# The query bias of a linear attention: from two products per batch on TensorE to operands of the ScalarE and VectorE maps

## What is computed

```python
q = _heads(hidden_states @ q_w.T + q_b, b, s)
k = _heads(hidden_states @ k_w.T + k_b, b, s)
v = _heads(hidden_states @ v_w.T + v_b, b, s)
qp = jax.nn.elu(q) + 1.0
kp = jax.nn.elu(k) + 1.0
kv = jnp.einsum('bhsd,bhse->bhde', kp, v)
z = jnp.einsum('bhsd,bhd->bhs', qp, kp.sum(axis=2))[..., None]
attn = jnp.einsum('bhsd,bhde->bhse', qp, kv) / (z + EPS)
out = attn.transpose(0, 2, 1, 3).reshape(b, s, HID)
return out @ o_w.T + o_b
```

## Time and profile before

| what | us |
|---|---|
| median of 3 runs | 138.21 |
| lowest, highest | 137.30, 138.31 |
| the profiled execution's own time | 135.21 |
| its span | 133.4 |
| TensorE busy in the span | 125.2 |
| VectorE, ScalarE, GpSimd busy | 80.9, 75.8, 71.0 |

### The profile page before, as it was taken

The page is one execution under the profiler, slowest core; times in us unless marked ns, Lnnn a source line. Parts: engine busy times, 40 slices in busy tenths (PEclk is TensorE's granted clock), DMA queues, the critical chain, the costliest instruction groups (busy, mean ns, idle before and its releaser), DMA issues.

```text
span 133.4 us, 2624 instructions
## 1 busy us (share of the span) xinstructions
PE 125.2 (94%) x975; PEld 116.9 (88%) x975; DVE 80.9 (61%) x205; ACT 75.8 (57%) x162; POOL 71.0 (53%) x90
## 2 busy tenths in 40 slices
PE   6989797999899999999999999999999999999980
PEld 2249696999899999889999989999989999999980
DVE  0269985789986895857786696564635413324122
ACT  4168579595676589568543982654397530355300
POOL 3015999959999998855270352650226440144600
PEclk9999999999999999999999999999999999999999
DMA  3899976000000000000000200000200000200002
GB/s 69 231 387 374 396 244 227 5 0 2 2 5 0 0 2 5 0 0 0 5 0 0 79 0 5 2 0 0 82 1 0 2 0 5 79 0 0 5 0 79
DMA packets 4721, 7.64 MB, mean 57 GB/s; under 512 B 608, under 2 KB 2592, under 8 KB 4580
## 3 DMA queue, kind: packets, MB, share of 16 engines
q1 hardware_dynamic: 4478, 7.37, 16.1%
q10 hardware_dynamic: 230, 0.11, 0.5%
HBM read 6.42 MB, written 1.05 MB: 56 GB/s over the span
## 4 chain that ended last, share of the span: by engine, by line
PE 76%; DVE 6%; DMA 4%; SPq 3%; POOL 3%; ACT 2%; issue 2%; POOLq 0%; DVEq 0%
PE bank L1123 35%; PE bank L1136 17%; PE bank L1001 5%; PE bank L1087 4%; DMA at<-in_mask_key 4%; PE bank L1025 3%; PE bank L1109 3%; PE bank L1049 2%; PE bank L1059 2%; PE bank L1095 1%; PE bank L1069 1%; ACT mbias L396 1%; POOL at L280 1%; PE bank L992 1%; DVE st L647 1%
## 5 line engine op out<-in xcount | busy, mean ns | idle before, releaser
L1123 PE MATMUL bank<-xh_home,wug 128*128 128x256 f32 x384 | 49.5, 285 | 0.0
L1123 PEld LDWEIGHTS bank<-xh_home,wug 128*128 128x128 f32 x384 | 47.2, 190 | 0.5 <-issue 0.4
L311 POOL TENSOR_TENSOR hs<-front,hs 128x256 fp32r<-128x256 f32 x32 | 24.1, 761 | 32.6 <-ACT hs L530 32.6
L521 ACT ACTIVATE front<-bank,vecs 128x256 f32<-128x256 f32 x32 | 15.0, 473 | 18.6 <-PE bank L1123 18.5
L822 DVE SCALAR_TENSOR_TENSOR front<-bank,sc_up,front 128x256 f32<-128x256 f32 x32 | 15.2, 480 | 16.1 <-ACT front L521 16.1
L1136 PE MATMUL bank<-wdh,hs 128*128 128x256 f32 x192 | 23.8, 283 | 0.0
L1136 PEld LDWEIGHTS bank<-wdh,hs 128*128 128x128 f32 x192 | 23.4, 191 | 0.1
L530 ACT CAST hs<-front 128x256 fp32r<-128x256 f32 x32 | 12.8, 400 | 5.5 <-DVE front L822 5.4
L1025 PE MATMUL bank<-wqkv,xT 128*128 128x256 f32 x96 | 14.2, 289 | 0.0
L1025 PEld LDWEIGHTS bank<-wqkv,xT 128*128 128x128 f32 x96 | 12.3, 189 | 0.6 <-DVE xT L689 0.4
L647 DVE BATCH_NORM_STATS2 st<-x_res 128x6 f32<-128x256 f32 x24 | 9.1, 416 | 5.2 <-DMA x_res<-in_x 5.0
(11 more groups left out here) (105 smaller groups left out, 194.9 us busy)
## 6 DMA issues: line engine op xcount, KB each, us to landing
wd_a<-in_w_d SPq DMA_DIRECT2D x1, 1024.0 KB, 8.6
front<-in_w_ug SPq DMA_DIRECT2D x2, 512.0 KB, 9.8
back<-in_w_ug SPq DMA_DIRECT2D x2, 512.0 KB, 5.3
out<-x_res SPq DMA_DIRECT2D x8, 128.0 KB, 1.9
wd_b<-in_w_qkv SPq DMA_DIRECT2D x3, 256.0 KB, 5.6
x_res<-in_x SPq DMA_DIRECT2D x1, 512.0 KB, 6.8
back<-in_ctx_t SPq DMA_DIRECT2D x1, 260.0 KB
x_res<-in_x SPq DMA_DIRECT2D x2, 128.0 KB, 3.3
```

Source lines behind the costliest of these rows:

```text
L311: g.tensor_tensor(hs[:, 1, n % JB, :], sg[:, n % RING, :], hs[:, 0, n % JB, :].bitcast(F32), ALU.subtract)\
L521: a.activation(sg[:, n % RING, :], B("GU", n)[:, 0:SEQ], ACT.Silu, scale=vecs[:, V_WSUG + JB + j:V_WSUG + JB + j + 1]).then_inc(s["sg"], 1)
L1123: ins = mm(dst[:, n * SEQ:(n + 1) * SEQ], wug[:, wa, k, at_col + j * P:at_col + (j + 1) * P], xh[b][:, xb, k, :], start=(i == 0), stop=(i ...
```

## The change

The seventh product for each block of queries goes, and with it the query half of the bias rows and their split. The query bias arrives as two more columns of the tile `vecs`, and `vector_sums` on VectorE (which takes the place of `scale_up`, at an earlier point) makes two tiles of 128 x 2 from it, -q_b and q_b + 1. ScalarE now makes three instructions of `exp_q` instead of one: for each block m a Relu of -q - q_b from the bank into `eq`, then, after a wait for both, the exponential of the negated `eq` in place. This is exp(min(q + q_b, 0)). VectorE makes two instructions of `elu_q` instead of one: for each block m the maximum of `eq` and bank + (q_b + 1).

```diff
-V_SUG, V_SUD, V_WSUG, V_COLS = 0, 2, 10, 26
-
-K_COLS, Q_COLS = slice(0, HID), slice(HID, 2 * HID)
+V_SUG, V_SUD, V_WSUG, V_QB, V_COLS = 0, 2, 10, 26, 28
...
+        qb_minus = sb("qb_minus", [P, FB])
+        qb_plus = sb("qb_plus", [P, FB])
         rows = sb("rows", [P, 3, HID])
-        bias_r = sb("bias_r", [BIAS_ROWS, 2 * HID], F32R)
-        ones = sb("ones", [BIAS_ROWS, HID], F32R)
+        bias_r = sb("bias_r", [BIAS_ROWS, HID], F32R)
+        ones = sb("ones", [BIAS_ROWS, P], F32R)
...
-                a.activation(eq[:, :], B("Q", b)[:, :], ACT.Exp, bias=neg1[:, :]).then_inc(s["eq"], 1)
+                    act.wait_ge(s["q_bias"], 1)
+                for m in range(FB):
+                    cols = slice(m * SEQ, (m + 1) * SEQ)
+                    a.activation(eq[:, cols], B("Q", b)[:, cols], ACT.Relu, bias=qb_minus[:, m:m + 1], scale=-1.0).then_inc(s["q_neg"], 1)
+                act.wait_ge(s["q_neg"], FB * b + FB)
+                a.activation(eq[:, :], eq[:, :], ACT.Exp, scale=-1.0).then_inc(s["eq"], 1)
...
-            bias_hi(K_COLS)
+            bias_hi()
...
-            bias_hi(Q_COLS)
...
-                v.scalar_tensor_tensor(qT[:, b % 2, :, :], eq[:, :].rearrange("p (m s) -> p m s", m=FB), 1.0,
-                                       B("Q", b)[:, :].rearrange("p (m s) -> p m s", m=FB),
-                                       ALU.min, ALU.max).then_inc(read_of("Q", b), 1)
+                if b == 0:
+                    dve.wait_ge(s["q_bias"], 2)
+                for m in range(FB):
+                    cols = slice(m * SEQ, (m + 1) * SEQ)
+                    ins = v.scalar_tensor_tensor(qT[:, b % 2, m, :], B("Q", b)[:, cols], qb_plus[:, m:m + 1], eq[:, cols], ALU.add, ALU.max)
+                ins.then_inc(read_of("Q", b), 1)
...
-            def scale_up():
+            def vector_sums():
                 dve.wait_ge(ld["vec"], 16)
+                q_bias = vecs[:, V_QB:V_QB + FB]
+                v.tensor_scalar(qb_minus[:, :], q_bias, -1.0, None, ALU.mult).then_inc(s["q_bias"], 1)
+                v.tensor_scalar(qb_plus[:, :], q_bias, 1.0, None, ALU.add).then_inc(s["q_bias"], 1)
                 v.tensor_tensor(sc_up[:, :], vecs[:, V_WSUG:V_WSUG + JB], vecs[:, V_SUD:V_SUD + JB], ALU.mult).then_inc(s["sc_up"], 1)
...
-            bias_lo(0, K_COLS)
+            bias_lo()
             u_lo(0)
             xT_lo(0)
             w_lo(1)
             w_lo(2)
-            bias_lo(1, Q_COLS)
             ln_stats(1, 1)
+            vector_sums()
             elu_k(0)
             v_add(0)
             u_lo(1)
             ln_stats(1, 2)
-            scale_up()
             elu_q(0)
             xT_lo(1)
...
                 if b == 0:
                     pe.wait_ge(s["w_lo"], 3)
-                    pe.wait_ge(s["bias"], 2)
...
                     for n, (k, wa, xb) in enumerate(PASSES):
-                        mm(into, wqkv[:, wa, 2, k, m * P:(m + 1) * P], xT[:, b % 2, xb, k, :], start=(n == 0), stop=False)
-                    ins = mm(into, bias_r[:, HID + m * P:HID + (m + 1) * P], ones[:, :], start=False, stop=True)
+                        ins = mm(into, wqkv[:, wa, 2, k, m * P:(m + 1) * P], xT[:, b % 2, xb, k, :], start=(n == 0),
+                                 stop=(n == len(PASSES) - 1))
...
-        "bias": np.stack([b_kq, b_kq, np.ones(2 * HID, np.float32)]),
+        "bias": np.stack([b_k, b_k, np.ones(HID, np.float32)]),
...
-        "vec": np.concatenate([columns(a[n]) for n in ("L0_ffn_SU_ug", "L0_ffn_SU_dp", "L0_ffn_Wscale_ug")], 1),
+        "vec": np.concatenate([columns(a[n]) for n in ("L0_ffn_SU_ug", "L0_ffn_SU_dp", "L0_ffn_Wscale_ug", "L0_attn_q_b")], 1),
```

More of the change, by code:

```diff
@@ L178, in decoder_kernel @@
         qkv_raw = wd_b[:, 0:FB * 3, :].rearrange("p (c f) o -> p c f o", c=3)
-        bias_raw = kvs[0:BIAS_ROWS, :, :].rearrange("p b e -> p (b e)")[:, 0:2 * HID]
+        bias_raw = kvs[0:BIAS_ROWS, :, :].rearrange("p b e -> p (b e)")[:, 0:HID]
         bytes_of = at[:, :, :, :].rearrange("p two i d -> p (two i d)").bitcast(U8)
@@ L210, in decoder_kernel @@
                  "ug_hi ug_lo fly pre_hi pre_lo wd_hi "
-                 "xT_hi ek eq z_eps z_inv at_hi "
+                 "xT_hi ek q_neg eq q_bias z_eps z_inv at_hi "
                  "sx logit prob rsum x2 y "
@@ L379, in bias_rows @@
             def bias_rows():
-                a.mul(ones[:, :], neg1[0:BIAS_ROWS, :].to_broadcast([BIAS_ROWS, HID]), -1.0).then_inc(s["ones"], 1)
+                a.mul(ones[:, :], neg1[0:BIAS_ROWS, :].to_broadcast([BIAS_ROWS, P]), -1.0).then_inc(s["ones"], 1)
                 act.wait_ge(s["bias_zero"], 1)
@@ L418, in w_hi, with bias_hi @@
                 a.copy(wqkv[:, 0, c], qkv_raw[:, c]).then_inc(s["w_hi"], 1)
-            def bias_hi(cols):
+            def bias_hi():
                 act.wait_ge(ld["bias"], 16)
-                a.copy(bias_r[:, cols], bias_raw[:, cols]).then_inc(s["bias_hi"], 1)
+                a.copy(bias_r[:, :], bias_raw).then_inc(s["bias_hi"], 1)
             def normalise(n, b, into):
@@ L656, in normalise1, with bias_lo @@
                                     ALU.subtract, ALU.mult).then_inc(s["xn1"], 1)
-            def bias_lo(n, cols):
+            def bias_lo():
                 low_row = slice(ROW_LO, ROW_LO + 1)
-                dve.wait_ge(s["bias_hi"], n + 1)
-                v.tensor_tensor(bias_r[low_row, cols], bias_raw[low_row, cols], bias_r[low_row, cols].bitcast(F32), ALU.subtract)\
+                dve.wait_ge(s["bias_hi"], 1)
+                v.tensor_tensor(bias_r[low_row, :], bias_raw[low_row, :], bias_r[low_row, :].bitcast(F32), ALU.subtract)\
                     .then_inc(s["bias"], 1)
@@ L1030, in kv_proj @@
                             pe.wait_ge(s["ones"], 1)
-                        ins = mm(into, ones[:, 0:P], bias_r[:, K_COLS], start=False, stop=True)
+                        ins = mm(into, ones[:, 0:P], bias_r[:, :], start=False, stop=True)
                 done(ins, name, b)
@@ L1178 @@
     eye, same = np.eye(HPB, dtype=np.float32), np.ones((HD, HD), np.float32)
-    b_kq = np.concatenate([a["L0_attn_k_b"], a["L0_attn_q_b"]])
+    b_k = a["L0_attn_k_b"]
     arrays = {
```

## The result

| | before | after |
|---|---|---|
| median of 20 runs each, us | 138.12 | 140.05 |
| the profiled execution, us | 135.21 | 137.71 |
| its span, us | 133.4 | 135.8 |
| TensorE busy, us | 125.2 | 124.4 |
| VectorE, ScalarE, GpSimd busy, us | 80.9, 75.8, 71.0 | 83.0, 78.4, 70.5 |

The ratio is 1.0153, with a 95% interval of 1.0142 to 1.0163. On executions of some 135.5 us this is +2.07 us.

The account below looks back on a forecast made before the run. The prediction took the head's chain across engines, then TensorE's gapless tail, to bound the kernel. `add_attn(0)` 1.77 us later, less 0.24 for Q(3), gave +1.53: 138.21 + 1.5 = 139.7 us, range 138.0 to 140.9.

Parts of the forecast that it names:

- What bounds it: A head of some 36 us, chained across engines, sets when TensorE's gapless tail starts; earlier TensorE savings count only on that chain.
- ScalarE's price: Two Relus, a wait and an exponential replace one exponential: +0.85 us from full bank Q to finished `eq`, bounds +0.49 to +1.29.
- VectorE's +0.19: In the query map on VectorE, one instruction of 0.68 us becomes two taking 0.87: +0.19 us, bounds zero to +0.28.
- TensorE's saving: Eight bias products go, 0.96 us of TensorE; only Q(1)'s and Q(3)'s count, -0.24 us each.
- Batch 0: In the head, the longer map delays `xT_lo(1)`, K(1), the mask instruction and the quotient: +1.04 us.
- the quotient, which had waited 1.10 us for the mask and had nothing else late: Last step for batch 0: the quotient follows the later mask instruction, so it moves by the same +1.04 us.
- Batch 1: In the head, the longer map ahead of `add_attn(0)`: +0.85 + 0.19 - 0.24 - 0.07 us, the query side alone last.
- Batch 2: `exp_q(2)` ahead of `xT_hi(3)`: the extra 0.85 us just fits into 0.33 + 0.6 of slack, so zero.
- Batch 3: In the gapless stretch, ScalarE's longer map costs zero and Q(3)'s missing products give -0.24 us.
- the nearest is WD(1): Of TensorE's next groups behind batch 3's map, WD(1) takes the tightest bank, with 0.70 us to spare against 0.35 and 0.24.
- rival B: Batch 2's or 3's 0.85 isn't absorbed, so TensorE's tail gets a new gap, up to 0.7 us more: 140.4; chance 0.10.
- Rival A: Not slower, delays in batches 0 and 1 covered: 137.7 us, or 138.7 half covered; chances 0.12 and 0.13.

Follow-up runs that it names:

- the two runs without the meeting: Changed kernel with the split of w_o moved earlier, or with GpSimd's butterfly(0,0) moved later; one undisturbed execution each, 136.94 and 136.85 us.

## Why the prediction came out as it did

- **What bounds it: right.** Less busy time on TensorE (-0.8 us) went with a longer span, through the head's chain. From `add_attn(0)` to T1(3) the stretch moved as a whole, 8.11 and 8.10 us.
- **ScalarE's price: right**, +0.81 for +0.85. VectorE's +0.19 was exact. TensorE's saving was right too: Q(1) and Q(3) take 0.26 us less each, for 0.24.
- **Batch 0: +1.04 forecast, +1.33 measured.** The mechanism was right and measures 0.98 by itself, as the two runs without the meeting show (the two prices add to 1.00). The step that failed is "the quotient, which had waited 1.10 us for the mask and had nothing else late". I took VectorE's own order behind `xT_lo(1)` to move unchanged, and it has 1.10 us of cover only while its instructions keep their durations. Moved by 1.3 us, the split of w_o came just behind the start of GpSimd's butterfly, where it had been 0.46 ahead, and took 1.73 us longer; the cover was used up and 0.35 came out. The sign that the prediction gave for being right, an idle time near 1.1 before the quotient, is gone.
- **Batch 1: +0.73 forecast (0.85 + 0.19 - 0.24 - 0.07), +0.65 measured**, and 0.64 alone. By its parts, behind the quotient: -0.25 until the map starts on ScalarE, +0.82 until it starts on VectorE, +0.08 from there to `add_attn(0)`. Overlap took 0.11 of VectorE's 0.19, where I had 0.07, a value for which I named no row.
- **Batch 2: zero, right**, and just so: `xT_hi(3)` stands 38.81 - 38.12 = 0.69 us behind T1(3), 0.70 before, and its idle time of 0.33 is used up.
- **Batch 3: -0.24 forecast, +0.10 measured.** The step that failed is "the nearest is WD(1)". I left 0.35 us of delay for ScalarE's work behind the map; 0.19 came. WD(1) lost some 0.2 us (its group takes 1.27 instead of 1.07), so even its 0.70 us to spare was too much: its second half began on the timeline before at 55.02 and not at 55.19. And the release that set the time was the next one: gate/up block 4 takes a bank that VectorE's quotient of batch 2 reads, and this had nothing to spare (it began 0.15 us behind the first of the pair, before and after). TensorE came there early by what it had saved and idled 0.31 us. This is the kind of gap that rival B names, at a bank that it doesn't name, and it happened; I had given it 0.10.
- **Rival A** would have needed the waits to be of another origin; `add_attn(0)` came at 30.02, not 27.7.

Forecast and result differ by 0.54 us: 0.35 from the meeting, 0.34 from batch 3, less 0.14 of small overestimates in batches 0 and 1 and 0.01 of rounding. The two missed terms together are 0.69 us, a third of the whole difference, and both could be seen in the profile of the kernel before: by the butterfly's 2.84 us beside 2.39, and by the 0.15 us ahead of block 4.

## What to carry to other kernels

An engine that is 94% busy isn't the one to relieve where a chain across other engines sets the start of its full stretch; price the edit by the latency between two neighbours of that chain. When an instruction order is shifted, look at what the other engine does at the new time: here an instruction with two operands in SBUF on VectorE couldn't be taken at its old duration, since GpSimd was at work there. A group that shows no idle time before it can still have nothing to spare: compare its start with the end of what releases it, and work that out for each group behind the change, not for the nearest alone. And where an instruction waits for a long one that needed nothing late itself, ask first whether the long one may go ahead: here exchanging two lines gave about 1 us, as much as all eight products of the change are worth (0.96 us).

## What the runs showed of the hardware

In these traces a VectorE instruction with both inputs in SBUF and a GpSimd instruction that reads SBUF don't run side by side: the one that starts first goes on, and the other takes longer by about what is left of the first. The split of w_o took 0.68 us when GpSimd wasn't in its way, 2.78 when it began 0.15 us behind a butterfly of 2.38, and when it began 0.07 us ahead it took 0.68 and the butterfly 2.86. Splits with one input in PSUM (L693 at 19.15, 0.68 us, beside GpSimd's instruction of 18.70 to 19.98) kept their time. The Trainium skill states this (SBUF — State Buffer, section Who interferes with whom): a VectorE instruction with two SBUF inputs contends with a GpSimd instruction that reads SBUF, as an exclusive lock; the traces agree, and the rule would have belonged in the prediction.

TensorE's granted clock stayed at 1.00 (2.4 GHz) through the head in seven of the fourteen profiles. In the other seven it fell to 0.50 (1.2 GHz) between 7.5 and 8.8 us and rose again between 14.7 and 17.8 us, and GpSimd's row of 15.3 is at 18.2 to 19.9. Shortly before the fall (in one profile across it) TensorE idled for 1.21 to 2.12 us until the context's load let it start at 7.1 to 7.7; in the profiles at full clock it idled there for 0.34 to 0.87 us, until 6.8 to 7.4. Whether this idle time is the cause, no run tested.
